# Two score steps share one round of maxima subtraction, and GpSimd sums the exponentials in two alternating buffers

## The reference, cut to what matters

```
q, k, v = einsum('bsm,hmd->bhsd', xn, kernel[0..2])
scores  = einsum('bhsd,bhtd->bhst', q, k) * scale
attn    = softmax(scores, axis=-1)
out     = einsum('bhst,bhtd->bhsd', attn, v), heads joined, times WO[0]
```

## Time and profile before

| | |
|---|---|
| median of three runs | 3418.86 us |
| the profiled execution | 3421.26 us, of which the span that the trace covers is 3419.4 |
| layer 0's attention | from about 236 to 1464 us of the span |
| layer 1's attention | from about 2080 to 3409 us |
| TensorE busy | 3133.3 us (92%) |
| GpSimd busy | 2394.8 us (70%) |
| VectorE busy | 2356.3 us (69%) |
| ScalarE busy | 1427.8 us (42%) |
| dearest group | GpSimd's adds, L847 (those onto `total`): 768 of 2364 ns |

### The profile page before, as it was taken

The page is one execution under the profiler, slowest core; times in us unless marked ns, Lnnn a source line. Parts: engine busy times, 40 slices in busy tenths (PEclk is TensorE's granted clock), DMA queues, the critical chain, the costliest instruction groups (busy, mean ns, idle before and its releaser), DMA issues. The chain is left out here.

```text
span 3419.4 us, 47107 instructions
## 1 busy us (share of the span) xinstructions
PE 3133.3 (92%) x18389; PEld 1247.1 (36%) x18389; DVE 2356.3 (69%) x3610; ACT 1427.8 (42%) x1609; POOL 2394.8 (70%) x1080
## 2 busy tenths in 40 slices
PE   5949999999999999948888985999999999999997
PEld 3414444444444444333333431333333333333333
DVE  6545555555555555351211696999999999999996
ACT  3325555555555555510000222555554555545544
POOL 0019999999999999900000383888888888888887
PEclk9969999999999999958888997999999999999998
DMA  3341111112111111010000133111111111112200
GB/s 80 126 123 26 25 26 26 26 26 49 26 26 26 26 26 25 1 51 0 0 0 0 49 148 97 49 49 49 49 49 49 49 49 49 49 54 60 60 23 13
DMA packets 53617, 148.69 MB, mean 43 GB/s; under 512 B 17155, under 2 KB 24076, under 8 KB 51220
## 3 DMA queue, kind: packets, MB, share of 16 engines
q1 hardware_dynamic: 53396, 145.67, 15.5%
HBM read 110.78 MB, written 34.87 MB: 43 GB/s over the span
## 5 line engine op out<-in xcount | busy, mean ns | idle before, releaser
L847 POOL TENSOR_TENSOR a_total<-a_total,room 128x1024 f32<-128x1024 f32 x768 | 1815.3, 2364 | 141.9 <-ACT room L740 37.3
L650 PE MATMUL a_ov<-room,va 128*64 128x512 f32 x4096 | 991.6, 605 | 0.0
L774 DVE TENSOR_REDUCE a_mx<-a_jb 128x1 f32<-128x1024 f32 x512 | 627.2, 1225 | 508.6 <-PE a_jb L613 508.6
L733 ACT ACTIVATE room<-room,sscale 128x1024 f32<-128x1024 f32 x512 | 588.4, 1149 | 650.5 <-DVE room L794 650.4
L740 ACT ACTIVATE room<-a_st,sscale 128x1024 f32<-128x1024 f32 x512 | 548.8, 1111 | 556.6 <-PE a_st L639 556.6
L769 DVE CUSTOM_DVE_ANT_0 a_junk<-a_jb,a_tab 128x1024 bf16<-128x1024 f32 x512 | 623.8, 1218 | 50.9 <-PE a_jb L613 34.6
L794 DVE TENSOR_TENSOR room<-a_st,a_tab 128x1024 f32<-128x1024 f32 x512 | 623.7, 1219 | 5.2 <-PE a_st L639 3.0
L612 PE MATMUL a_jb<-a_kh,a_qh 64*128 64x512 f16 x1024 | 396.6, 387 | 102.0 <-DMA a_tab<-bias_line 30.9
L847 POOL TENSOR_TENSOR a_total<-room 128x1024 f32<-128x1024 f32 x128 | 302.5, 2363 | 182.4 <-ACT room L733 135.6
L639 PE MATMUL a_st<-a_qh,a_kh 64*128 64x512 f16 x2048 | 394.9, 382 | 21.0 <-DVE room L794 21.0
L650 PEld LDWEIGHTS a_ov<-room,va 128*64 128x64 f32 x4096 | 248.4, 136 | 423.6 <-issue 363.7
(11 more groups left out here) (181 smaller groups left out, 2616.1 us busy)
## 6 DMA issues: line engine op xcount, KB each, us to landing
a_tab<-bias_line SPq DMA_DIRECT2D x16, 1984.0 KB, 12.1
qk_high<-q_oh SPq DMA_DIRECT2D x32, 512.0 KB, 2.6
qk_low<-q_ol SPq DMA_DIRECT2D x32, 512.0 KB, 3.6
a_qh<-qk_high SPq DMA_DIRECT2D x64, 256.0 KB, 4.9
a_kh<-qk_high SPq DMA_DIRECT2D x64, 256.0 KB, 5.7
a_ql<-qk_low SPq DMA_DIRECT2D x64, 256.0 KB, 6.3
a_kl<-qk_low SPq DMA_DIRECT2D x64, 256.0 KB, 6.7
ex_w<-in_L_ffn_W SPq DMA_DIRECT2D x1, 2048.0 KB, 10.5
```

Of the source, the lines that this page charges most:

```text
L650: last = nc.tensor.matmul(ov[t * DH:(t + 1) * DH, :], k.va[:, 2 * s + t, h * DH:(h + 1) * DH], prob[:, step % RING, t * QC:(t + 1) * QC], ...
L733: nc.scalar.activation(prob[:, r, :], prob[:, r, :], ACT.Exp, scale=k.sscale[:, layer:layer + 1])\
L774: nc.vector.reduce_max(mx[:, j // 2, j % 2:j % 2 + 1], jb[:, :], AX.X).then_inc(max_done, 1)
L847: nc.gpsimd.tensor_tensor(t, first, prob[:, step % RING, :], ALU.add).then_inc(summed, 1)
```

## The change

1. Layer 0 only: `scores` has three rounds. A new `subtract_maxima(n, s)` comes behind the scores of both steps of a pair and subtracts for both in one round of four products on 32-row tiles: quarter 0 and 2 of the array for step s (key block 0 and 1), quarter 1 and 3 for step s + 1. `st_ready` is raised for s behind the first two products, for s + 1 behind the last two.
2. For it `lower` has -128 in rows 0, 32, 64 and 96 in layer 0 (LOWERED = 4), still 0 and 64 in layer 1, and `m4w` gets the maxima in four columns in place of two, in both layers. Layer 1 keeps its four rounds.
3. Both layers: GpSimd has two sums and alternates. Add i = 0 is step 0 + 1 into one, i = 1 is step 2 + 3 into the other, i = 2 to 5 put steps 4, 5, 6, 7 in turn onto the one and the other (each waits for the add before the last, not for the last). A seventh add merges the two, and the fold writes to `total`, which has now one buffer of 512 and waits until the last projection has read it. `summed_by` follows the new order.

```diff
+LOWERED = (4, 2)
-        total = m.sb(g + "total", [P, 2, 2 * QC])
+        sums, total = m.sb(g + "sums", [P, 2, 2 * QC]), m.sb(g + "total", [P, QC])
-            return pool_adds * n + min(max(1, s), pool_adds)
+            return pool_adds * n + (1, 1, 2, 2, 3, 4, 5, 6)[s]
-                for r, (keys, queries) in enumerate(((kh, qh), (kh, ql), (kl, qh), (lower, rows))):
+                rounds = ((kh, qh), (kh, ql), (kl, qh)) + (((lower, rows),) if bias else ())
+                for r, (keys, queries) in enumerate(rounds):
...
-                last.then_inc(st_ready, 1)
+                if bias:
+                    last.then_inc(st_ready, 1)
+
+            def subtract_maxima(n, s):
+                for i in range(2):
+                    for t in range(2):
+                        quarter = slice((2 * t + i) * 32, (2 * t + i + 1) * 32)
+                        last = nc.tensor.matmul(st[:, (NS * n + s + i) % 2, t * QC:(t + 1) * QC], lower[quarter, :],
+                                                rows[quarter, n % 2, :], start=False, stop=True)
+                    last.then_inc(st_ready, 1)
...
                         scores(n, s)
                         scores(n, s + 1)
+                        subtract_maxima(n, s)
                         ahead(n, s + 1)
...
-                nc.scalar.activation(m4w[:, :, 0:DH + 1:DH], m4[:, :].unsqueeze(2).broadcast_to([P, 4, 2]), ACT.Copy,
+                nc.scalar.activation(m4w[:, :, ::32], m4[:, :].unsqueeze(2).broadcast_to([P, 4, 4]), ACT.Copy,
...
-            nc.gpsimd.memset(lower[0:1, :], -float(MAXROW)).then_inc(ones_set, 1)
-            nc.gpsimd.memset(lower[DH:DH + 1, :], -float(MAXROW)).then_inc(ones_set, 1)
+            for u in range(LOWERED[layer]):
+                nc.gpsimd.memset(lower[u * P // LOWERED[layer]:u * P // LOWERED[layer] + 1, :], -float(MAXROW))\
+                  .then_inc(ones_set, 1)
             for n in range(NCH):
-                t = total[:, n % 2, :]
-                if n >= 2:
-                    pool.wait_ge(proj_ready, 2 * (n - 1))
-                for s in range(1, pool_adds + 1):
+                for i, s in enumerate((1, 3, 4, 5, 6, 7)):
                     step = NS * n + s
+                    a = sums[:, (n + i) % 2, :]
                     pool.wait_ge(exp_done, step + 1)
-                    first = prob[:, (step - 1) % RING, :] if s == 1 else t
-                    if s >= 2:
-                        pool.wait_ge(summed, pool_adds * n + s - 1)
-                    nc.gpsimd.tensor_tensor(t, first, prob[:, step % RING, :], ALU.add).then_inc(summed, 1)
+                    if i >= 2:
+                        pool.wait_ge(summed, pool_adds * n + i - 1)
+                    if i == 1 and n >= 1:
+                        pool.wait_ge(folded, n)
+                    first = a if i >= 2 else prob[:, (step - 1) % RING, :]
+                    nc.gpsimd.tensor_tensor(a, first, prob[:, step % RING, :], ALU.add).then_inc(summed, 1)
+                pool.wait_ge(summed, pool_adds * n + 6)
+                a = sums[:, n % 2, :]
+                nc.gpsimd.tensor_tensor(a, a, sums[:, (n + 1) % 2, :], ALU.add).then_inc(summed, 1)
                 pool.wait_ge(summed, pool_adds * (n + 1))
-                nc.gpsimd.tensor_tensor(t[:, 0:QC], t[:, 0:QC], t[:, QC:2 * QC], ALU.add).then_inc(folded, 1)
+                if n >= 1:
+                    pool.wait_ge(proj_ready, 2 * n)
+                nc.gpsimd.tensor_tensor(total[:, :], a[:, 0:QC], a[:, QC:2 * QC], ALU.add).then_inc(folded, 1)
```

More of the change, by code:

```diff
@@ L666, in project @@
                     q = (2 * e + t) * P
-                    nc.tensor.matmul(xb[:, 2 * P + t:2 * P + t + 1], total[:, n % 2, q:q + P], k.ones[:, 0:1],
+                    nc.tensor.matmul(xb[:, 2 * P + t:2 * P + t + 1], total[:, q:q + P], k.ones[:, 0:1],
                                      start=(t == 0), stop=True, skip_group_check=True)
@@ L673, in project @@
                 last.then_inc(proj_ready, 1)
-            pe.wait_ge(ones_set, 2)
+            pe.wait_ge(ones_set, LOWERED[layer])
             for j in range(NJ):
@@ L747, in copy_out @@
                 nc.scalar.activation(osb[:, :], ov[:, :], ACT.Copy).then_inc(ov_saved, 1)
-            act.wait_ge(ones_set, 2)
+            act.wait_ge(ones_set, LOWERED[layer])
             divide_maxima(0)
@@ L806, in accumulate @@
                 last.then_inc(proj_done, 1)
-            ve.wait_ge(ones_set, 2)
+            ve.wait_ge(ones_set, LOWERED[layer])
             for j in range(NJ):
```

## The result

The changed kernel takes 3447.41 us (median of four runs, 3444.58 to 3450.18), the kernel before 3418.25 (3417.58 to 3419.49): 1.0085 of it, 95% interval 1.0067 to 1.0102. That is 29.2 us slower; the forecast was 3447. The profiled execution took 3445.91, at the lower end of its runs, with a span of 3444.1: 24.7 over the span of before.

What follows compares the result with a forecast made beforehand. Layer 0 was bound by TensorE's own work; the loop would grow 0.74 + 1.96 against 2.29 slack, to 19.44 us a chunk: +29.6, less 0.9 in layer 1, +28.7 on the median 3418.86, so 3447; range 3434 to 3474.

Steps and rivals of the forecast that it cites:

- The loop and the wait: Layer 0: exponential of step 4, GpSimd's adds, fold, next projection, scores; 19.44 us a chunk, TensorE waiting 0.4 to 0.5.
- The shift of the exponential: Layer 0, step 4: the exponential starts 0.74 us later, behind both steps' score rounds; projection to exponential 4.99.
- The switches: Layer 0, TensorE: two tile-shape changes in each of four pairs, 0.10 us each, 0.80 a chunk; own work 18.97.
- rival A: Layer 0: the tile switch is free; loop 19.34 us, +23.3, 3441; chance 14%.
- B: Layer 0: TensorE becomes its own bound with a dearer four-tile round; about 19.8 us a chunk, +52, 3470; chance 17%.
- the 0.20 of the earlier trace: Upper bound in us for one tile switch, from where an 8-row operand meets 128 rows in the profile before.
- GpSimd's tail: Layer 0, add 4 through merge to the fold's end: 13.16 us, 13.26 with handover; +1.96 on the loop.
- One of the signs named in advance: Layer 0, changed profile: GpSimd idles 1 to 1.5 us ahead of step 4's add.
- Rival C: Layer 0: GpSimd's tail stays short, so the kernel gets faster; middle chunk 18.6 us, -26, 3393; chance 10%.
- E: GpSimd: the adds keep their gaps, 2.50 us apart; loop 19.98, 35 more than the forecast, 3482; chance 4%.
- The ends: Layer 0's first and last chunks: 19.22 us for chunks 62 and 63, no extra for chunk 0.
- Layer 1: Second attention stage: chunks unchanged, 2.6 us of slack hidden under VectorE; 0.9 us gained at the last chunk.

Runs made afterwards that it cites:

- the first experiments: Follow-ups starting with each half alone in place of the whole change: GpSimd's sums 3423.18 us, the shared round 3423.43, against 3419.96 of the kernel before.
- The fold done twice: The changed kernel with layer 0's fold executed two times, same values, the second raising `folded`: 3547.35 us in a single run, against 3418.91 of the kernel before.

## Why the prediction was right

**The loop and the wait** were right, and shown: undoing either half, moving the projection, or shortening the tail each brings the chunk back to 19.03 to 19.06 and the time to within 1.0 to 3.5 us of before; lengthening the tail by 1.34 lengthens the chunk by 1.34.

**The shift of the exponential** (+0.74): from projection to step 4's exponential 4.98 us, forecast 4.99.

**The switches**: taken as 0.10 from the 64-to-128-row rows, because no row had 64 to 32. Measured 0.31 - 0.215 = 0.095 into the 32-row round and 0.33 - 0.215 = 0.11 out of it, if the four tiles together last as long as one round of two. They don't run two by two, which would take 0.43; how much of the 0.11 is the switch and how much the four tiles no run tells apart. The Trainium skill says ("TensorEngine Tiling (Array Packing)", Key Properties) that a change of tiling mode drains TensorE. The trace agrees for these switches: time is lost at both, and none (0.21) where the round keeps its 64 rows. TensorE's own chunk is 19.04 where the sum had 18.97. Rivals A and B fall, and the 0.20 of the earlier trace rows was the wrong neighbour. The measured chunk of 19.34 is the figure of rival A, but not for A's reason: the switch on the loop costs its 0.1, and the difference to 19.44 lies in GpSimd's tail.

**GpSimd's tail** was mis-sized by 0.09: 13.07 for 13.16 to the fold's end. The four adds took 9.30 (forecast 9.32), but the gap ahead of the merge is 0.08 (723.46 - 723.38), not the 0.14 of the dependent adds of before. So the chunk is 19.34, not 19.44, and the wait 0.3, not 0.4 to 0.5. One of the signs named in advance missed: GpSimd idles 1.64 us ahead of step 4's add, not 1 to 1.5. The terms of the sum would have given it (19.44 - 13.16 - 4.64 = 1.64), so it was misread from them and is no fault of the mechanism. Rival C needed a loop of 19.03; E needed gaps that stay; both fall.

**The ends** were mis-sized the other way. I had 19.22 for chunks 62 and 63 and nothing for chunk 0; they take 20.76, 20.79 and 20.99, since I had not asked how long TensorE would wait there, nor what the clock does behind such a wait (0.83 in the windows above). Taken together: 60 chunks at 0.10 under the forecast are -6.0, the three ends are +1.5 to +1.6 each. The interval that the sum was made for, add 4 of chunk 0 (248.27) to the last projection (1484.41), is 1236.1 us, forecast 1237.5. Part of that closeness is two errors against each other.

**Layer 1** was right in the main: all but a few chunks are 20.33 to 20.36 in both profiles. From layer 0's last projection to the last fold of the kernel it is 1942.45 us after and 1943.51 before, 1.1 less, forecast 0.9. That the two agree is luck again. The 0.9 stood for the last two chunks, with a bound of 1.8; they are 18.64 and 17.65 after, 19.68 and 18.68 before, 2.07 less. The first chunk is 0.39 longer (19.81 for 19.42) and it takes 0.5 more to reach the first fold, which the sum had at nothing and no run explains.

**The total.** 27.9 us of the difference stand in layer 0, of the 24.7 of the spans; 2.1 go back because the stage began 2.1 us earlier in this execution (first score round at 235.76, before at 237.84), and 1.1 in layer 1. The 2.1 are chance as far as the runs show: in the nine profiles of all versions that start lies anywhere from 235.29 to 239.39. So the sum, which was made within one profile, forecast +28.7 where the two profiles differ by 24.7, and that the median met the forecast to 0.4 us, among runs that spread over 5.6, is luck in good part. The changed kernel's four runs spread over 5.6 us and the four of before over 1.9, but that is no sign of the change: on the chip of the first experiments 31 runs of the kernel before spread over 6.4 (3416.91 to 3423.34).

## What to carry to other kernels

Ask of each wait how long its chain is around the loop, not only how full its engines are: here two edits that each fit in 2.29 us of slack (0.73 and 1.87) didn't fit together, and no engine's busy time shows it. A reduction that is split into two running sums moves a merge behind the last item, on the path of whoever waits for the result; here the work saved in front of it was in the shade. And a round of small tiles between rounds of larger ones pays for two switches, here 0.2 us, which is just what a saved round of 512 columns brings (0.215).

## What the runs showed of the hardware that was not expected

- The gap between GpSimd operations that depend on each other is not one number: 0.14 us from add to add where each reads the one before (kernel before), 0.08 ahead of the merge and of the fold, which do so too (changed kernel), and an overlap of 0.04 where the result before is not read. The cause is open. The number of waits isn't it, as far as these rows go: the add of before and the fold of the changed kernel both have two in the program, the merge and the second fold of "The fold done twice" have one, with the same 0.08.
- The same wait of 1.60 us in every chunk was followed by a lower granted clock in only one chunk of eight or nine (22.33 us against 20.68). Behind the waits of 1.33 and 2.19 at the ends of the changed kernel's stage the window has 0.83; behind 1.11 at the same place with half of the merge left out it has 1.00, and behind waits of 0.26 no chunk was longer. No run shows what decides it.
